# Attention and gated scan on one core: the broadcast of 1/l issued in two halves, the second behind the swap of step 3

## The chip, the core and the metric

The kernel runs on one core of a Trainium2 chip. The metric is the device time of one execution in microseconds (us); the figure given for the kernel before is the median of three executions. Besides it there is one profiled execution, from which every duration of single instructions is taken. The engines are TensorE (PE, with PEld for its weight loads), VectorE (DVE), ScalarE (ACT), GpSimd (POOL) and SyncE (SP), which here only issues DMAs.

## The reference

A batch of 32 sequences of 256 tokens with 128 features passes through two layers, each with a residual.

```python
x = x + attention(layernorm(x), norm_weight, w_qkv, w_out, persist_mem)
x = x + ffn(layernorm(x), ...)
# attention: rms_norm, q, k, v = h @ w_qkv.T, 16 heads of 64, rope on q and k,
# 4 persistent keys and values ahead of the 256, causal softmax, out @ w_out.T
# ffn: over the 32 batches in order,  c = sigmoid(..) * c + sigmoid(..) * tanh(..)
#      h = tanh(x @ wo.T + c_final @ uo.T + bo)
```

The softmax is divided by its row sum l only at the end: the unnormalised product of exp(scores) and v is multiplied by 1/l. The change concerns how 1/l reaches the place of that multiplication.

## The kernel before, in words

**Work and order.** The Python loop `iterations` (L202) runs `body(j, p)` for j = 0 to 34 on each engine, so that each engine has a fixed list of instructions, ordered by hand; engines meet through semaphores only. One iteration has eight steps s = 0 to 7, one for each pair of heads. In iteration j the engines project batch j, do the scores, the softmax and the values of batch j - 1 and j, divide and project out batch j - 2, and run the scan for batch j - 3.

**Rope, one pair of heads a step.** `project` (PE, L1021) makes q and k of one pair in the one PSUM bank `ps_proj`; it waits until DVE has read the pair before. `rotate` (DVE, L793) multiplies the bank by cos into `rope_a` (L798) and by sin into `rope_b` (L799). `rope_b` and `rope_c` have two buffers each, by s % 2. `swap` (SP, L287) waits for the `rope_b` of its step and issues two DMAs that copy the even rows of `rope_b` to the odd rows of `rope_c` and the other way (128 KB each). `rope_add` (POOL, L403) waits for the swap and adds `rope_a` and `rope_c` to `qk`; in the order of POOL the add of pair s - 1 stands in step s, ahead of `prob_add` (L396). `hi` (ACT, L524) casts `qk` to `qk_h`, from which `scores_for_max` (PE, L1060) makes the scores whose row maxima `maxima` (DVE, L801) takes; for pairs 0 to 4 of batch j these run in steps 3 to 7 of iteration j. `transpose_top` (PE, L1077) of step 7 waits for the maxima of step 6. `rotate` of step s waits for the swap of step s - 2 (L797), because it writes the same `rope_b` buffer. So `rotate` of step 5 waits for the landing of the swap of step 3.

**1/l.** In step 1 `invert` (DVE, L828) takes the reciprocal of the row sums of batch j - 2 (L832). In step 2 SP runs `store_linv` (L296), which stores it to a DRAM scratch tensor in two DMAs of 64 KB, then the swap of step 2, then `spread_linv` (L303), which waits for the store to land and for the divisions of the batch before, and issues four DMAs of 256 KB each that read the scratch tensor and write each head's 1/l to the 64 partitions of that head in `rinv`. The first two fill pairs 0 to 3 of `rinv` (semaphore `spread0`), the other two pairs 4 to 7 (`spread1`). The swap of step 3 comes behind the four. `divide` (DVE, L834) multiplies `raw` by `rinv` for two pairs at a time (L845): its first two parts in step 4, behind `spread0`, its last two in step 5, behind the `rotate` of that step and behind `spread1`. `project_out` (PE, L1172) follows in steps 5 and 6. The last batch gets its 1/l through PE (`spread_last`), so there are 31 broadcasts, in iterations 2 to 32; in iteration 32 there is no swap.

**SP's order** in steps 2 and 3 is thus:

```python
if c and s == 2 and j - 2 < NB - 1:
    store_linv(j - 2)
if a:
    swap(j, s)
if c and s == 2 and j - 2 < NB - 1:
    spread_linv(j - 2)
```

After the swap of step 3 comes `tails` (L315), a DMA of 8 KB with the persistent values, and then the swap of step 4. From ACT's queue one batch of x (128 KB) is loaded in each step 4 (L473).

Of the kernel before, what the change touches and what calls it, by code (L numbers as in the profile page):

```python
# [5 lines left out]
NB, NT, D = 32, 256, 128  # L6
# [38 lines left out]
def wait(eng, sem, count):  # L45

    if isinstance(count, int) and count <= 0:
        return
    eng.wait_ge(sem, count)


def build(nc, x, x_last, w_qkv_t, w_out_t, norm_w, pm_k, pm_v, ffn_w, ffn_b, bo_row, consts_f32, consts_cast,
# [9 lines left out]
    with ctx:  # L62
        def sb(name, shape, dt):
            return ctx.enter_context(nc.sbuf_tensor(name, shape, dt))
# [76 lines left out]
        rinv = sb("rinv", [P, NPAIR, NT], f32)  # L141
# [14 lines left out]
        linv_dram = nc.dram_tensor("linv_scratch", [2, 32, 2, NT], f32, kind="Internal").ap()  # L156
# [23 lines left out]
        spread = [S[f"spread{i}"] for i in range(2)]  # L180
# [17 lines left out]
        def real(b):  # L198

            return not isinstance(b, int) or 0 <= b < NB  # L200

        def iterations(eng, body):  # L202


            for j in range(NB + 3):
                body(j, j % 2)

        OWN = (slice(0, 64), slice(64, 128))
# [32 lines left out]
        def fin_x(g):  # L241
            return x_sb[:, FB * g:FB * g + FB, :]
# [20 lines left out]
        @block.sync  # L263
        def _(sp):
            def const_f32(t, name):
                return sp.dma_start(t, consts_f32[:, C32[name][0]:C32[name][1]])

            def load_x(i):
                lo, hi = XCH[i], XCH[i + 1]
                sp.dma_start(x_sb[:, lo:hi, :].rearrange("p b (q d) -> p b q d", q=QT),  # L270
                             x_d[:, lo:hi, :, :]).then_inc(ld_x[i], 16)

            sp.dma_start(x_end[:, :], x_last).then_inc(S["ld_end"], 16)
            load_x(0)
            const_f32(ident_f[:, :], "ident").then_inc(S["ld_ident"], 16)
            sp.dma_start(nw[:, :], norm_w).then_inc(S["ld_ident"], 16)
            sp.dma_start(bias_raw[:, :], ffn_b).then_inc(S["ld_ident"], 16)
            const_f32(cos[:, :], "cos").then_inc(S["ld_rope"], 16)
            const_f32(sin[:, :], "sin").then_inc(S["ld_rope"], 16)
            sp.dma_start(c_raw, consts_cast).then_inc(S["ld_c"], 16)  # L280
            sp.dma_start(pmk_raw[:, :], pm_k).then_inc(S["ld_small"], 16)
            sp.dma_start(bo_sb[:, :], bo_row).then_inc(S["ld_small"], 16)
            const_f32(ones_sum[:, :, :].rearrange("p c n -> p (c n)"), "ones_sum").then_inc(S["ld_small"], 16)
            const_f32(ones_end[:, :, :].rearrange("p e n -> p (e n)"), "ones_end").then_inc(S["ld_small"], 16)
            load_x(1)

            def swap(j, s):  # L287

                sp.wait_ge(S["qk_read"], NPAIR * j + s + 1)
                sp.sem_inc(S["sp_tick"], 1)  # L290
                wait(sp, S["rope_sum"], NPAIR * j + s - 1)
                sp.sem_inc(S["sp_tick"], 1)
                for i in range(2):
                    sp.dma_start(rope_c[i::2, s % 2, :], rope_b[1 - i::2, s % 2, :]).then_inc(swapped[s % 2], 16)

            def store_linv(cj):  # L296

                sp.wait_ge(S["linv_done"], cj + 1)
                sp.sem_inc(S["sp_tick"], 1)
                for b in range(2):  # L300
                    sp.dma_start(linv_dram[:, :, b, :], linv[OWN[b], :]).then_inc(S["linv_stored"], 16)

            def spread_linv(cj):  # L303

                sp.wait_ge(S["linv_stored"], 32 * (cj + 1))
                sp.sem_inc(S["sp_tick"], 1)
                wait(sp, S["norm_done"], 4 * cj)
                sp.sem_inc(S["sp_tick"], 1)
                for half in range(2):
                    for e in range(2):  # L310
                        src = linv_dram[e:e + 1, 2 * half:2 * half + 2, :, :].rearrange("o k b n -> o (k b n)")
                        sp.dma_start(rinv[OWN[e], 4 * half:4 * half + 4, :].rearrange("p s n -> p (s n)"),  # L312
                                     src.to_broadcast([64, 4 * NT])).then_inc(spread[half], 16)

            def tails(bj, half):  # L315

                col = half * DI // 2
                sp.wait_ge(S["v_done"], 4 * bj + 2 * half + 1)
                sp.sem_inc(S["sp_tick"], 1)
                sp.dma_start(v_sb[0:NPM, 0, col:col + DI // 2], pm_v[:, col:col + DI // 2]).then_inc(v_pm[half], 16)  # L320

            def tail_values(bj):

                wait(sp, S["pv_ready"], NPAIR * bj)
                sp.sem_inc(S["sp_tick"], 1)
                if bj == 0:
                    sp.wait_ge(S["ve_stored"], 16)
                    sp.wait_ge(S["casts_pool"], 14)
                for half in range(2):
                    src = v_end_dram[NEND * bj:NEND * bj + NEND, half * DI // 2:(half + 1) * DI // 2]  # L330
                    sp.dma_start(v_end[HB * half:HB * half + KE, :],
                                 src.rearrange("k (s n) -> s k n", s=NPAIR // 2)).then_inc(S["v_end"], 16)

            def body(j, p):
                a, b, c = real(j), real(j - 1), real(j - 2)
                for s in range(NPAIR):
                    if c and s == 2 and j - 2 < NB - 1:
                        store_linv(j - 2)
                    if a:
                        swap(j, s)  # L340
                    if c and s == 2 and j - 2 < NB - 1:
                        spread_linv(j - 2)
                    if j == 1 and s == 3:
                        sp.wait_ge(S["ve_copied"], 2)
                        sp.dma_start(v_end_dram, raw[:, 1, 0:4, :].rearrange("p c n -> p (c n)")).then_inc(S["ve_stored"], 16)
                    if b and s == 3 and j < NB:
                        tails(j - 1, 1)
                    if b and s == 5:
                        tail_values(j - 1)
                    if a and s == 6:  # L350
                        tails(j, 0)

            iterations(nc.sync, body)
            for g in range(NB // FB):
                sp.wait_ge(S["fin_out"], g + 1)
                sp.dma_start(out_d[:, FB * g:FB * g + FB, :, :],
                             fin_x(g).rearrange("p b (q d) -> p b q d", q=QT)).then_inc(S["stored"], 16)
            sp.wait_ge(S["stored"], 16 * (NB // FB))
# [1093 lines left out]
```

## Time and profile before

| what | value |
|---|---|
| median of three executions | 1133.06 us (1131.0 to 1133.95) |
| the profiled execution's own time | 1133.03 us |
| its span in the profile | 1131.2 us |
| mean granted TensorE clock | 0.988 of full speed |
| PE, DVE, ACT, POOL busy | 95%, 82%, 62%, 56% of the span |
| DMA traffic | 120.52 MB, mean 107 GB/s |

A row of the timeline gives the start in us from the start of the span, the duration in us, the engine, the line, the operation with output and inputs, and the number of instructions merged into it; in square brackets stands how long the engine had been idle before it and what released it. SPq is SyncE's queue of DMA instructions: its durations are those of issuing, and the time to landing is told apart. The windows give the length of each window and the busy time of PE, PEld, DVE, ACT and POOL with the number of instructions, then PE's clock, the DMA share and GB/s. A row of the waits gives the total in us, the number of times and the longest. L numbers are lines of the kernel.

### The profile page before, as it was taken

To read this page: it belongs to the slowest core of one execution; us is meant where nothing else is said; L and a number is where in the kernel's file an instruction comes from. 1 tells how busy PE (TensorE), PEld (TensorE's weight loads), DVE (VectorE), ACT (ScalarE), POOL (GpSimd) and SP (SyncE) were. 2 spreads that over 40 slices of the span, in tenths; PEclk is the share of its full clock that TensorE was granted. 3 is DMA by queue.
4 is the path that set the end of the run, shared out by engine and by line. 5 is a ranking of instruction groups with operands and counts; after the bars stand their busy time and mean duration, and the time that the engine had idled before them with its cause. 6 is when DMAs were issued, how large, how long until landed. Compare 5 with 4: busy or idle time off the path is not lost.

```text
span 1131.2 us, 47261 instructions
## 1 busy us (share of the span) xinstructions
PE 1080.3 (95%) x18443; PEld 813.6 (72%) x18443; DVE 930.0 (82%) x3305; ACT 698.4 (62%) x1575; POOL 634.8 (56%) x816
## 2 busy tenths in 40 slices
PE   3879999999999999999999999999999999999996
PEld 2457777777777776777777777677777777777784
DVE  5778888888888888888888888788888888888745
ACT  3556666666666666666666666666665666666644
POOL 3545665576565647656555665555565565556420
PEclk8889999999999999999999999999999999999999
DMA  6213343332333442233333233333323333332215
GB/s 204 95 62 112 111 115 114 115 95 89 111 111 114 115 114 90 90 111 115 115 115 115 83 100 115 107 114 115 115 78 98 114 115 111 108 112 92 68 36 150
DMA packets 78031, 120.52 MB, mean 107 GB/s; under 512 B 13041, under 2 KB 35954, under 8 KB 77682
## 3 DMA queue, kind: packets, MB, share of 16 engines
q1 hardware_dynamic: 68714, 111.20, 32.5%
q10 hardware_dynamic: 9096, 6.30, 2.1%
q8 instruction: 147, 2.41, 1.0%
q14 instruction: 74, 0.61, 0.2%
HBM read 41.56 MB, written 8.78 MB: 45 GB/s over the span
## 4 chain that ended last, share of the span: by engine, by line
PE 59%; DVE 16%; DMA 14%; SPq 4%; issue 3%; POOL 2%; ACT 1%; DVEq 0%; POOLq 0%
PE bank_pv L1142 11%; PE bank L1034 11%; DMA rope_c<-rope_b 10%; PE bank_st L1098 8%; PE bank_sum L1179 5%; PE bank_sum L1163 4%; DVE masked L809 4%; PE bank_sm L1073 4%; PE bank L1056 3%; DMA linv_scratch<-linv 3%; SPq L312 3%; DVE linv L832 2%; DVE rope_a L798 2%; PE bank L1281 2%; PE bank L1283 2%
## 5 line engine op out<-in xcount | busy, mean ns | idle before, releaser
L407 POOL TENSOR_TENSOR qk<-rope_a,rope_c 128x512 f32<-128x512 f32 x256 | 341.0, 1332 | 312.9 <-DMA rope_c<-rope_b 288.9
L809 DVE CUSTOM_DVE_ANT_0 masked<-bank_sm,mask_q 128x132 bf16<-128x132 f32 (+1 forms) x1024 | 307.1, 355 | 17.7 <-PE bank_sm L1073 17.2
L798 DVE TENSOR_TENSOR rope_a<-bank,cos 128x512 f32<-128x512 f32 x256 | 174.1, 680 | 130.1 <-PE bank L1034 83.7
L400 POOL TENSOR_TENSOR prob<-prob 128x264 f32<-128x264 f32 x256 | 210.8, 823 | 117.1 <-ACT prob L544 108.3
L529 ACT ACTIVATE qk_h<-qk 128x512 f16<-128x512 f32 x256 | 160.4, 627 | 172.2 <-POOL qk L407 171.7
L544 ACT ACTIVATE prob<-bank_st 128x784 f32<-128x784 f32 x256 | 209.3, 817 | 59.7 <-PE bank_st L1107 58.9
L1142 PE MATMUL bank_pv<-prob,v_sb 128*64 128x256 f32 (+1 forms) x2048 | 224.8, 340 | 0.6 <-DVE raw L825 0.6
L1098 PE MATMUL bank_st<-qk 64*64 64x256 f32 (+3 forms) x4096 | 186.3, 299 | 0.4 <-issue 0.2
L1098 PEld LDWEIGHTS bank_st<-qk 64*64 64x64 f32 x4096 | 167.7, 134 | 9.6 <-issue 1.3
L799 DVE TENSOR_TENSOR rope_b<-bank,sin 128x512 f32<-128x512 f32 x256 | 173.8, 679 | 0.0
L1142 PEld LDWEIGHTS bank_pv<-prob,v_sb 128*64 128x64 f32 x2048 | 124.3, 136 | 54.4 <-issue 0.9
L1034 PE MATMUL bank<-h_hi,w_hi 128*128 128x256 f16 x512 | 143.5, 280 | 5.8 <-DVE rope_b L799 5.0
L1034 PE MATMUL bank<-h_hi,w_lo 128*128 128x256 f16 x512 | 141.8, 277 | 0.0
L1034 PE MATMUL bank<-h_lo,w_hi 128*128 128x256 f16 x512 | 141.6, 277 | 0.0
L1179 PE MATMUL bank_sum<-wo_sb,raw 128*128 128x128 f32 x992 | 122.7, 276 | 0.0
L1179 PEld LDWEIGHTS bank_sum<-wo_sb,raw 128*128 128x128 f32 x992 | 116.0, 192 | 1.9 <-DVE raw L845 1.1
L578 ACT ACTIVATE v_sb<-bank 128x512 f32<-128x512 f32 x128 | 75.8, 593 | 48.2 <-PE bank L1053 28.7
L569 ACT ACTIVATE raw<-bank_pv 128x256 f32<-128x256 f32 x256 | 97.7, 382 | 4.1 <-PE bank_pv L1148 3.1
L845 DVE SCALAR_TENSOR_TENSOR raw<-rinv,raw 128x512 f32<-128x512 f32 x124 | 96.6, 819 | 2.0 <-DMA rinv<-linv_scratch 1.8
L1073 PEld LDWEIGHTS bank_sm<-qk_h 64*64 64x64 f16 x2048 | 37.6, 105 | 82.7 <-issue 56.6
L1073 PE MATMUL bank_sm<-qk_h 64*64 64x68 f16 (+3 forms) x2048 | 86.7, 246 | 4.4 <-ACT qk_h L529 3.1
L809 DVE DVE_READ_ACCUMULATOR2_ANT top<- 128x1 bf16 x1024 | 85.7, 84 | 0.1
(237 smaller groups left out, 1732.1 us busy)
## 6 DMA issues: line engine op xcount, KB each, us to landing
rope_c<-rope_b SPq DMA_DIRECT2D x512, 128.0 KB, 2.3
rinv<-linv_scratch SPq DMA_DIRECT2D x124, 256.0 KB, 4.8
out<-x_sb SPq DMA_DIRECT2D x16, 256.0 KB, 3.7
linv_scratch<-linv SPq DMA_DIRECT2D x62, 64.0 KB, 2.1
x_sb<-x ACTq DMA_DIRECT2D x28, 128.0 KB, 5.5
xt<-w_qkv_t ACTq DMA_DIRECT2D x1, 1024.0 KB, 5.3
v_end<-v_end_scratch SPq DMA_DIRECT2D x64, 8.0 KB
v_sb<-pm_v SPq DMA_DIRECT2D x63, 8.0 KB
```

The lines of the kernel that those rows point to most:

```text
L400: G.tensor_tensor(prob_2[:, s % 4, :, :], prob[:, s % 4, :, 0:NT - Q1], prob[:, s % 4, :, C0 + Q1:SCOL], ALU.add).then_inc(S["prob_added"], 1)
L407: G.tensor_tensor(qk[:, s, :].rearrange("p (u n) -> p u n", u=2)[:, :, 0:NT], rope_a[:, (NPAIR * j + s) % 3, :].rearrange("p (u n) -> p u ...
L529: A.activation(qk_h[:, s, :].rearrange("p (u n) -> p u n", u=2)[:, :, 0:NT], qk[:, s, :].rearrange("p (u n) -> p u n", u=2)[:, :, 0:NT], A ...
L544: A.activation(prob[:, s % 4, :, :], ps_st[:, :, 0:SCOL], ACT.Exp).then_inc(S["exp_done"], 1)
L798: V.tensor_tensor(rope_a[:, (NPAIR * j + s) % 3, :], proj_bank(j, s)[:, :], cos[:, :], ALU.mult)
L799: V.tensor_tensor(rope_b[:, s % 2, :], proj_bank(j, s)[:, :], sin[:, :], ALU.mult).then_inc(S["qk_read"], 1)
L809: ins = V.tensor_tensor_reduce(masked[:, e, c0:c0 + n], ps_sm[:, e, c0:c0 + n], mask_q[:, c0:c0 + n], 1.0, LOWEST, ALU.add, ALU.max, top[: ...
L1034: last = T.matmul(proj_bank(j, s)[:, u * NT:(u + 1) * NT], W[q][:, col:col + P], H[p][:, par, NPM:NKEY], start=(i == 0), stop=(i == 2))
L1073: last = T.matmul(ps_sm[OWN[SIDE[qb]], e, c0:c0 + n], qk_h[OWN[e], s, qb * HB:qb * HB + HB], qk_h[OWN[e], s, NT:NT + n], start=True, stop= ...
L1098: T.matmul(ps_st[OWN[SIDE[kb]], e, st_cols(blk)], qk[OWN[e], s, NT + kb * HB:NT + kb * HB + HB], qk[OWN[e], s, q0:NT], start=(kc == 0), st ...
L1142: last = T.matmul(ps_pv[OWN[e], q0:NT], v_sb[:, kc, col:col + DH], prob[:, s % 4, e, c0:c0 + NT - q0], start=(kc == 0), stop=(kc == 1))
L1179: last = T.matmul(y_out(cj)[:, q * D:(q + 1) * D], raw[:, par, s, q * P:(q + 1) * P], wo_sb[:, s, :], start=(alone and s == 0 and q == 0), ...
```

## The change

`spread_linv` gets a second argument, `half`, and issues only the two DMAs of that half. SP calls it twice in an iteration: for half 0 behind the swap of step 2, as before, and for half 1 behind the swap of step 3. Both calls keep the two waits and the two semaphore increments. The number of DMAs, their sizes, their semaphores and every other engine's program are the same.

```diff
-            def spread_linv(cj):
+            def spread_linv(cj, half):
 
                 sp.wait_ge(S["linv_stored"], 32 * (cj + 1))
                 sp.sem_inc(S["sp_tick"], 1)
                 wait(sp, S["norm_done"], 4 * cj)
                 sp.sem_inc(S["sp_tick"], 1)
-                for half in range(2):
-                    for e in range(2):
-                        src = linv_dram[e:e + 1, 2 * half:2 * half + 2, :, :].rearrange("o k b n -> o (k b n)")
-                        sp.dma_start(rinv[OWN[e], 4 * half:4 * half + 4, :].rearrange("p s n -> p (s n)"),
-                                     src.to_broadcast([64, 4 * NT])).then_inc(spread[half], 16)
+                for e in range(2):
+                    src = linv_dram[e:e + 1, 2 * half:2 * half + 2, :, :].rearrange("o k b n -> o (k b n)")
+                    sp.dma_start(rinv[OWN[e], 4 * half:4 * half + 4, :].rearrange("p s n -> p (s n)"),
+                                 src.to_broadcast([64, 4 * NT])).then_inc(spread[half], 16)
...
                     if a:
                         swap(j, s)
-                    if c and s == 2 and j - 2 < NB - 1:
-                        spread_linv(j - 2)
+                    if c and s in (2, 3) and j - 2 < NB - 1:
+                        spread_linv(j - 2, s - 2)
```

## Rows read from the trace of the kernel before

**Rows 1.** The page: busy tenths of PE in 40 slices of the span.

```profile
PE   3879999999999999999999999999999999999996
```

**Rows 2.** Busy time by window, one iteration each, from reciprocal to reciprocal.

```profile
408.79:443.76 34.97, 32.81 (x569) 24.64 (x568) 28.77 (x103) 21.09 (x49) 19.94 (x25) 1.00 0.36 101
509.08:541.63 32.55, 32.52 (x572) 24.73 (x568) 27.90 (x105) 21.07 (x49) 19.74 (x25) 1.00 0.37 112
```

**Rows 3.** Timeline of DVE: the reciprocal that opens iterations 2 and 31.

```profile
80.30 1.75 DVE L832 RECIPROCAL linv<-bank_sum 128x256 f32<-128x256 f32 x1
...
1037.35 1.75 DVE L832 RECIPROCAL linv<-bank_sum 128x256 f32<-128x256 f32 x1
```

**Rows 4.** Waits: DVE, 80.3 to 1037.3; SP, whole span; DVE, 1068 to 1089.

```profile
DVE rope_a L798 <- DMA rope_c<-rope_b: 41.8, 29, 3.1
...
SPq L306 <- DMA linv_scratch<-linv: 13.9, 31, 2.0
...
DVE raw L845 <- DMA rinv<-linv_scratch: 1.4, 1, 1.4
```

**Rows 5.** Timeline of SP's queue in the iteration that opens at 509.08.

```profile
512.25 1.13 SPq L294 DMA_DIRECT2D rope_c<-rope_b  x2
513.70 2.40 SPq L312 DMA_DIRECT2D rinv<-linv_scratch  x4
516.28 2.19 SPq L294 DMA_DIRECT2D rope_c<-rope_b  x2
519.18 6.14 SPq L294 DMA_DIRECT2D rope_c<-rope_b  x4
```

**Rows 6.** Timeline of DVE and PE, the same iteration.

```profile
514.74 0.68 DVE L799 TENSOR_TENSOR rope_b<-bank,sin 128x512 f32<-128x512 f32 x1
...
522.77 0.69 DVE L798 TENSOR_TENSOR rope_a<-bank,cos 128x512 f32<-128x512 f32 x1 [1.24 <-DMA rope_c<-rope_b]
523.98 1.84 DVE L845 SCALAR_TENSOR_TENSOR raw<-rinv,raw 128x512 f32<-128x512 f32 x2
...
530.18 0.11 PEld L1081 LDWEIGHTS bank_sm<-ident_b,top 128*128 128x128 bf16 x2 [0.18 <-DVE top L809]
```

**Rows 7.** DVE, PE: first, three latest, last of 29 rotations of step 5.

```profile
93.93 0.69 DVE L798 TENSOR_TENSOR rope_a<-bank,cos 128x512 f32<-128x512 f32 x1 [1.71 <-DMA rope_c<-rope_b]
...
424.91 0.69 DVE L798 TENSOR_TENSOR rope_a<-bank,cos 128x512 f32<-128x512 f32 x1 [2.98 <-DMA rope_c<-rope_b]
...
426.26 0.28 PE L1034 MATMUL bank<-h_hi,w_hi 128*128 128x256 f16 x1 [1.32 <-DVE rope_b L799]
...
722.76 0.69 DVE L798 TENSOR_TENSOR rope_a<-bank,cos 128x512 f32<-128x512 f32 x1 [3.13 <-DMA rope_c<-rope_b]
...
854.85 0.69 DVE L798 TENSOR_TENSOR rope_a<-bank,cos 128x512 f32<-128x512 f32 x1 [2.27 <-DMA rope_c<-rope_b]
...
1017.99 0.69 DVE L798 TENSOR_TENSOR rope_a<-bank,cos 128x512 f32<-128x512 f32 x1 [0.61 <-DMA rope_c<-rope_b]
```

**Rows 8.** By line: the DMAs to `rinv`, over the span.

```profile
L312 SPq DMA_DIRECT2D rinv<-linv_scratch x124: 467/597/1810, 84.9 to 1074.8; - x124
...
DMA to landing us min/median/max: 3.5/4.8/6.9
```

**Rows 9.** By line: the swaps of steps 2 and 3, same iteration.

```profile
L294 SPq DMA_DIRECT2D rope_c<-rope_b x2: 488/542/596, 512.2 to 512.8; - x2
...
DMA to landing us min/median/max: 2.0/2.0/2.1
...
L294 SPq DMA_DIRECT2D rope_c<-rope_b x2: 599/1073/1547, 516.3 to 517.9; - x2
...
DMA to landing us min/median/max: 4.8/4.9/5.1
```

**Rows 10.** Busy time in a window of 1 us of the same iteration.

```profile
517.00:518.00 1.00, 1.00 (x10) 0.30 (x7) 0.85 (x3) 1.00 (x3) 0.83 (x1) 1.00 1.13 254
```

**Rows 11.** Timeline of SP's queue, the iteration that opens at 408.79.

```profile
415.13 2.40 SPq L312 DMA_DIRECT2D rinv<-linv_scratch  x4
```

## The prediction

> **What bounds the kernel now.** I read the page first: PE is at nine tenths or more in 36 of 40 slices [rows 1], so a change to a queue of DMAs can only win where PE stands still. The next view is busy time by window, with the reciprocal of step 1 (L832) as the mark of an iteration. A quiet iteration lasts 32.55 us and holds 32.52 us of PE; its clock column reads 1.00, the upper level of 2.4 GHz. The iteration from 408.79 lasts 34.97 us with hardly more PE work in it, 32.81 [rows 2]. So 32.55 is PE's floor, and what stands above it is waiting. From the first mark at 80.30 to the one at 1037.35 there are 29 iterations [rows 3]: 957.05 us, against 29 x 32.55 = 943.95. The excess is **13.1 us**, 1.2% of the time, and it is all that the steady part has to give.
>
> The waits of DVE say where it arises. `rope_a` of L798 waits for the DMA into `rope_c` 29 times in these 29 iterations, 41.8 us in all [rows 4]: once in each, at the rotation of step 5, which needs the swap of step 3. In SP's queue that swap stands behind four broadcast DMAs [rows 5]. Its `rope_b` was done at 514.74 + 0.68 = 515.42 [rows 6], but it was issued only at 516.28, and landed 4.8 to 5.1 us after issue where the swap of step 2 took 2.0 [rows 9]: ahead of it lie 4 x 256 KB, and the 16 DMA engines are full (share 1.13, 254 GB/s) [rows 10]. It lets the rotation of step 5 go at 522.77, 13.69 us into the iteration [rows 2, 6].
>
> Is that late enough for PE? From the rotation DVE goes on to two divisions at 523.98, a cast and the maxima, and PE's transpose at 530.18 waits 0.18 us for them [rows 6]: just at the edge. I took the start of the step-5 rotation less the mark for each of the 29 iterations, and set it beside each iteration's length. They fit one line: nothing up to 13.86 us, then one us of length for each us of lateness. The three latest are 424.91 - 408.79 = 16.12, 722.76 - 706.39 = 16.37 and 854.85 - 839.40 = 15.45 [rows 2, 7] (the marks 706.39 and 839.40 are read as those of [rows 3]), with 2.26, 2.51 and 1.59 above 13.86; the first of these shows 2.42 above the floor by its window [rows 2]. In it PE also waits openly, 1.32 us at L1034 for DVE's `rope_b` [rows 7]. Summed over all 29 (the first is 93.93 - 80.30 = 13.63, the last 13.32) the part above 13.86 is **12.4 us** of the 13.1. The other 0.7 comes before step 5 or from elsewhere, and the change does not touch it.
>
> **The change, part by part.** *The swap of step 3 moves up.* Half 0 keeps its place: two of four issues, half of 2.40, so 1.20 us from 513.70 to 514.90 [rows 5]. SP then waits for `rope_b` until 515.42 and issues at about 515.6 instead of 516.28, 0.7 us earlier. Ahead of it are 512 KB less; at 254 GB/s [rows 10] that is 2.1 us. It should land some 2.8 us earlier, 10.9 us into a quiet iteration, and in the three late ones at 12.7 to 13.6, all under 13.86. The rotation of step 5 then waits for PE's projection alone, which ended 1.24 us before it in the quiet iteration [rows 6]. So this part alone is worth the whole 12.4.
>
> *Half 1 moves down.* Its two issues come behind the swap (1.13 us, as that of step 2 [rows 5]) and start at about 515.6 + 1.13 + 0.15 = 516.9 instead of 514.9, 2.0 us later; the second starts 0.6 us after the first, at 517.5, 8.4 us into the iteration. Who waits is the division of step 5, on DVE behind the rotation, and behind it the cast, the maxima and the rotation of step 6. In the kernel before it starts 1.21 us after the rotation [rows 6], so its own edge is 13.86 + 1.21 = **15.07 us** into the iteration: what half 1 lands later than that costs one for one. The trace does not show that landing in the new order, so I bound it. Low end: the median of the broadcasts, 4.8 us from issue [rows 8], gives 8.4 + 4.8 = 13.2 in a quiet iteration and at most 14.5 in one whose store of 1/l was late: no cost. High end: the longest of the broadcasts, 6.9 us [rows 8], in every iteration: 15.3 to 16.6, over 29 iterations 14.1 us. I take a value between, from the nearest row: the same bytes (four broadcasts and one swap) go through the same full engines, only in another order, so the last of them lands when the last landed before, and that was the swap of step 3, whose landing is the start of the step-5 rotation. The 29 starts against 15.07 leave 1.05 + 1.30 + 0.38 = **2.7 us**, from the three latest alone [rows 7].
>
> *Also moved past on SP's queue.* The small `tails` DMA and the swap of step 4 (519.18 [rows 5]) come after the same number of issues as before; SP reaches them at the same time, and the swap waits for its `rope_b` anyway. POOL's and ACT's work behind the swap of step 3 gets earlier, which frees nothing on PE. The second call adds two waits that are already met and two semaphore increments, some 0.1 us of SP, which is idle for most of an iteration: nothing. It also looks once more at the store of 1/l (13.9 us of waiting in 31 times before [rows 4]); the first call has waited for it, so the second never does. That wait is why the broadcast starts 6.34 us into the iteration at 408.79 [rows 11] against 4.62 [rows 5], and it stays. In iteration 32 there is no swap, the four DMAs go out in a row as before, and DVE's 1.4 us there [rows 4] stays.
>
> *A rule to weigh.* The rows of the broadcasts and swaps show the swap slow behind four broadcasts and quick without them, as if the queue were served in order. The Trainium skill, page "DMA: Bandwidth & Descriptors", section "Two DMAs through the same engine are not ordered", says that descriptors start in order but are pipelined, and that nothing orders DMAs across the 16 engines. By the first reading half 1 cannot delay a swap issued ahead of it; if the second went so far that all five DMAs ended together, the swap would gain nothing, which is the first rival.
>
> The sum: 12.4 - 2.7 = 9.7 us off the profiled execution, 1133.03 - 9.7 = 1123.3 us. That execution lies 0.03 us below the median of the three runs, so no correction is needed.
>
> **The rivals.** A measurement of this kernel can tell about 0.3%, or 3.4 us, from no change.
>
> *The burst lands as one.* Half 1 follows the swap within 0.2 us and shares all DMA engines; if they mix, the swap lands with the last of the burst, as before, and the excess stays: 1133. For it: the engines are full, and the swap of step 4 already shares them. Against it: the swap of step 3 lands later than the broadcasts issued before it. Between this and the forecast lies a part: swap and half 1 both middling late.
>
> *Everything goes.* Half 1 lands by the median, the 2.7 us vanish too: 1133.0 - 12.4 = 1120.6.
>
> *Slower: half 1 becomes the late one.* The wait moves from L798 to L845 on DVE, and the maxima and PE's transpose follow. It decides from the landing of half 1's second DMA: at 6.9 us from issue the loss of 14.1 is 1.7 more than the gain of 12.4, so break-even is a little under that. At 7.4 us, half a us over the longest seen, it costs 29 x 0.99 = 28.7, net 16.3: 1149. For it: it is issued 2.0 us later into engines that are already full, and the swap of step 4 and the load of x come close behind. Against it: the bytes ahead of it grow only by a swap, and those behind it in the queue came late before, too.
>
> *The change does nothing*, because half 1 was never ahead of the swap in effect, is excluded by the rows: four issues stand before it [rows 5].
>
> **How the numbers follow.** Forecast with half 1's leftover between 0 and about 6 us, 1120.5 to 1126.5, "everything goes" among it: 0.70 (of this the lower end, 1120.6, 0.25). Gain between 3.4 and 6 us: 0.07. Burst as one, or a part gain within 3.4 us, or half 1 at the longest landing (1134.7): 0.15. Slower: 0.08. So faster 0.77, same 0.15, slower 0.08. The predicted time is that of the likeliest, 1123.3. The range begins at 1119.8, just under the floor of 1120.6 by what single runs scatter, and must reach past the part gains to 1129.6, where the 0.3% ends; 0.77 lies inside, and a little more for the edge: 1119.8 to 1130.0.
>
> **What would show it.** Right: in SP's queue two broadcasts, a swap 6.5 us into the iteration, two broadcasts; the rotation of step 5 at about 12.5 us, released by PE; the wait of L798 for `rope_c` down from 41.8 us to near nothing; a wait of L845 for `rinv` in few iterations, of a few us in all; 29 iterations in some 946 to 948 us. Wrong: L798 still released by the swap in most iterations (burst as one), or L845 waiting for `rinv` in most and the transpose of L1081 waiting behind it (slower). If the 29 iterations still take over 953 us with both waits gone, the line of 13.86 us was not the cause of the excess.

## The result and the profile after

The changed kernel is not faster but, by a small margin that is clear of the scatter, slower: 1135.46 us in the median of 20 runs (1131.27 to 1139.43) against 1131.98 us of the kernel before in 20 runs (1129.68 to 1134.92), a ratio of 1.0026 with an interval of 1.0013 to 1.0038. The forecast was 1123.3 us, and the range ended at 1130.0.

The profiled execution of the changed kernel happens to be the fastest of its 20, 1131.27 us with a span of 1129.5. A second one was taken in the first experiment.

The page, busy shares of the engines:

```profile
PE 1082.0 (96%) x18443; PEld 815.3 (72%) x18443; DVE 956.6 (85%) x3305; ACT 703.9 (62%) x1575; POOL 631.5 (56%) x816
```

PE does what it did. VectorE runs the same 3305 instructions and is busy for 956.6 us; on the page of before it was 930.0 (82%). Nothing was added to VectorE's program, and yet 26.6 us of busy time came in. That is the first thing to look at.

The waits of DVE from 80.3 to 1037.3 us, which answer to [rows 4]:

```profile
DVE raw L844 <- DMA rinv<-linv_scratch: 6.8, 11, 1.0
DVE rope_a L797 <- DMA rope_c<-rope_b: 0.9, 2, 0.7
```

The wait that the prediction went after is gone, 41.8 us down to 0.9, and the new wait for half 1 is small, 11 times and 6.8 us. Both are as forecast. Still the 29 iterations between the first and the last mark, which answer to [rows 3], take 954.19 us against 957.05:

```profile
80.19 1.75 DVE L831 RECIPROCAL linv<-bank_sum 128x256 f32<-128x256 f32 x1
...
1034.38 1.75 DVE L831 RECIPROCAL linv<-bank_sum 128x256 f32<-128x256 f32 x1
```

That is 10.2 us above the floor of 29 x 32.55 (the excess of the prediction), and this is the best execution. In the second profiled one it was 12.8, and 13.1 in the kernel before. The prediction had named this sign: over 953 us with both waits gone, and lateness past its line of 13.86 us is not the cause of the excess. Indeed the step-5 rotations are late by only 4.9 us in all beyond that line, read as in the prediction, against 12.4 before.

SP's queue in the iteration that opens at 377.20, the answer to [rows 5]:

```profile
383.70 1.13 SPq L294 DMA_DIRECT2D rope_c<-rope_b  x2
385.01 1.11 SPq L311 DMA_DIRECT2D rinv<-linv_scratch  x2
...
387.29 1.13 SPq L294 DMA_DIRECT2D rope_c<-rope_b  x2
```

And the landing of the second DMA of the swap of step 3 and of half 1, by line in windows that hold one DMA each, the answer to [rows 8, 9]:

```profile
L294 SPq DMA_DIRECT2D rope_c<-rope_b x1: 597/597/597, 384.2 to 384.2; - x1
DMA to landing us min/median/max: 4.9/4.9/4.9
...
L311 SPq DMA_DIRECT2D rinv<-linv_scratch x1: 597/597/597, 385.5 to 385.5; - x1
DMA to landing us min/median/max: 6.3/6.3/6.3
```

The swap goes out 6.50 us into the iteration and lands at 384.2 + 4.9 = 389.1, 11.9 us in; half 1 lands at 385.5 + 6.3 = 391.8, 14.6 us in, just before its edge of 15.07. So the queue does what the change says. The order was kept where it mattered: the swap was complete 2.7 us before the half that was issued behind it, and in all 29 iterations it was so by 1.7 us or more. Over the 29 the swap is complete 11.8 us into the iteration on average (14.0 before) and half 1 at 14.5; half 1 passes 15.07 in six of them, by 2.4 us in all.

What DVE and GpSimd did with it, timelines of the same iteration put together in order of time, the answer to [rows 6]:

```profile
388.17 1.28 DVE L844 SCALAR_TENSOR_TENSOR raw<-rinv,raw 128x512 f32<-128x512 f32 x2
389.27 1.31 POOL L406 TENSOR_TENSOR qk<-rope_a,rope_c 128x512 f32<-128x512 f32 x1 [3.62 <-DMA rope_c<-rope_b]
389.38 1.49 DVE L903 SCALAR_TENSOR_TENSOR c<-ga,gb 128x256 f32<-128x256 f32 x1
390.54 0.93 POOL L399 TENSOR_TENSOR prob<-prob 128x264 f32<-128x264 f32 x1
390.79 0.68 DVE L797 TENSOR_TENSOR rope_a<-bank,cos 128x512 f32<-128x512 f32 x1
391.39 0.68 DVE L798 TENSOR_TENSOR rope_b<-bank,sin 128x512 f32<-128x512 f32 x1
391.98 2.36 DVE L844 SCALAR_TENSOR_TENSOR raw<-rinv,raw 128x512 f32<-128x512 f32 x2
392.43 1.36 POOL L406 TENSOR_TENSOR qk<-rope_a,rope_c 128x512 f32<-128x512 f32 x1 [0.96 <-DMA rope_c<-rope_b]
```

The swap lands, GpSimd starts its rope add at 389.27, and the state update of the scan (L903) that VectorE starts 0.11 us later lasts 1.49 us. The rotation of step 5 shows no wait: it stands behind that update, and begins at 390.79, 13.59 us into the iteration, hardly before the 13.69 of the quiet iteration in [rows 6]. The two divisions behind it take 2.36 us with the next rope add beside them, where the undisturbed pair at 388.17 takes 1.28. The same operations grouped by line and shape, from 80.3 to 1037 us, of the kernel before and then of the changed one (count, busy us, mean ns, idle before them):

```profile
L845 DVE SCALAR_TENSOR_TENSOR raw<-rinv,raw 128x512 f32<-128x512 f32 x116 | 90.5, 821 | 0.5 <-DMA rinv<-linv_scratch 0.4
...
L904 DVE SCALAR_TENSOR_TENSOR c<-ga,gb 128x256 f32<-128x256 f32 x28 | 11.6, 415 | 0.0
```

```profile
L844 DVE SCALAR_TENSOR_TENSOR raw<-rinv,raw 128x512 f32<-128x512 f32 x116 | 100.1, 903 | 7.2 <-DMA rinv<-linv_scratch 6.8 <-issue 0.2
L903 DVE SCALAR_TENSOR_TENSOR c<-ga,gb 128x256 f32<-128x256 f32 x28 | 26.1, 934 | 0.0
```

The update went from 415 to 934 ns, the division from 821 to 903. The rotation, which reads its first input from PSUM, is 680 ns before and 678 after, though GpSimd runs beside it too (`prob_add` at 390.54).

### The profile page after: what moved, and what is told of

It is laid out like the page before. It is cut to its first block, busy times and chain, and to the rows that moved or that the text cites. A ratio compares the mean times of both kernels' runs of the same rounds, so it can differ in the third digit from the quotient of the medians.

```text
span 1129.5 us, 47323 instructions
## 1 busy us (share of the span) xinstructions
PE 1082.0 (96%) x18443; PEld 815.3 (72%) x18443; DVE 956.6 (85%) x3305; ACT 703.9 (62%) x1575; POOL 631.5 (56%) x816
## 4 chain that ended last, share of the span: by engine, by line
PE 73%; DVE 16%; DMA 4%; issue 3%; SPq 1%; POOL 1%; ACT 1%; DVEq 0%; POOLq 0%
PE bank_pv L1141 14%; PE bank L1033 13%; PE bank_st L1097 10%; PE bank_sum L1178 7%; PE bank_sum L1162 5%; PE bank_sm L1072 5%; DVE masked L808 4%; PE bank L1055 4%; DVE raw L844 3%; PE bank L1280 3%; PE bank L1282 3%; PE bank L1052 2%; PE bank_st L1101 2%; DVE rope_a L797 2%; DMA v_sb<-pm_v 2%
## 5 line engine op out<-in xcount | busy, mean ns | idle before, releaser
L399 POOL TENSOR_TENSOR prob<-prob 128x264 f32<-128x264 f32 x256 | 207.7, 811 | 142.5 <-ACT prob L543 136.1
L798 DVE TENSOR_TENSOR rope_b<-bank,sin 128x512 f32<-128x512 f32 x256 | 173.7, 678 | 0.0
L844 DVE SCALAR_TENSOR_TENSOR raw<-rinv,raw 128x512 f32<-128x512 f32 x124 | 106.5, 898 | 8.3 <-DMA rinv<-linv_scratch 8.0
```

The lines of the kernel that those rows point to most:

```text
L399: G.tensor_tensor(prob_2[:, s % 4, :, :], prob[:, s % 4, :, 0:NT - Q1], prob[:, s % 4, :, C0 + Q1:SCOL], ALU.add).then_inc(S["prob_added"], 1)
L798: V.tensor_tensor(rope_b[:, s % 2, :], proj_bank(j, s)[:, :], sin[:, :], ALU.mult).then_inc(S["qk_read"], 1)
```

## The experiments

Two theories stood after this. **Port theory:** the rope add of pair 3 on GpSimd, set free early, holds up VectorE operations that read two tensors from SBUF, the memory that both engines work on, and these stand ahead of the rotation. (The name is that of a supposed cause, a shared way into that memory; the runs can show the hold-up, not the port.) **Late-half theory:** half 1 is what costs. All edits are to the changed kernel unless said otherwise.

**The changed kernel again** (no edit).

> The changed kernel as it is, for a second profiled execution and as the control of this call. Both theories: within 1131 to 1139 us, some 0.3% above the kernel before. Port theory (GpSimd's rope add of pair 3 now runs while VectorE divides and updates the scan state, and the one holds up the other): the state update of step 4 (L903) has a mean of 900 ns or more against 415 before, and the rotation of step 5 starts at 13.5 us or later in most iterations though its swap has landed. Late-half theory (half 1 lands too late for the division of step 5): VectorE waits for rinv at L844 in most iterations, over 10 us in all.

Measured: 1133.99 us (12 runs), ratio 1.0019, 0.9999 to 1.0038. The state update has 934 ns again, and the step-5 rotation starts 13.66 us into an iteration on average (14.15 in the kernel before), in 19 of 29 iterations at 13.5 or later. VectorE waited for `rinv` 10 times, 7.4 us. This is the port theory on every count; the wait for the late half stays under the 10 us that its theory asked for.

**GpSimd held until the state update is done.**

```diff
+                    if s == 4 and real(j - 3) and a:
+                        pool.wait_ge(S["dve_s"], 3 * (j - 3) + 3)
                     if s >= 1 and a:
                         rope_add(j, s - 1)
```

> The changed kernel with one more wait: GpSimd starts the rope add of step 4 only when VectorE has finished the state update of step 4. Port theory: the state update falls back to 415 to 450 ns, the rotation of step 5 starts at 12.4 to 12.7 us, the excess over 32.55 us an iteration falls to 2 to 5 us, and the time to 1122 to 1126 us, 0.6 to 0.9% under the kernel before. Late-half theory: the excess stays at 10 to 14 us and the time at 1133 to 1137, for nothing is done about the landing of half 1.

Measured: **1125.69 us** (7 runs), ratio 0.9949, 0.9927 to 0.9971. One more wait makes the kernel faster. By line:

```profile
L905 DVE SCALAR_TENSOR_TENSOR c<-ga,gb 128x256 f32<-128x256 f32 x28 | 11.6, 413 | 0.0
```

By wait, 80.3 to 1037.3 us:

```profile
DVE raw L846 <- DMA rinv<-linv_scratch: 16.5, 25, 1.6
```

The update is back at 413 ns and the rotation starts at 12.78 us on average, a little later than the 12.4 to 12.7 forecast. Now that VectorE is early it does wait for `rinv`, 25 times, nearly always for half 1; but the excess, 7.6 us, is more than the 2 to 5 forecast, and the divisions of step 5 still last up to 2.9 us for the pair. The time lies inside the forecast, near its upper end.

**No half 1** (its two DMAs left out, the last two divisions read the first half).

```diff
-                    if c and s in (2, 3) and j - 2 < NB - 1:
-                        spread_linv(j - 2, s - 2)
+                    if c and s == 2 and j - 2 < NB - 1:
+                        spread_linv(j - 2, 0)
...
-                if n % 2 == 0:
-                    dve.wait_ge(spread[n // 2], 32 * (cj + 1))
-                V.scalar_tensor_tensor(o, rinv[:, 2 * n:2 * n + 2, :], 1.0, o, ALU.mult, ALU.mult).then_inc(S["norm_done"], 1)
+                if n == 0:
+                    dve.wait_ge(spread[0], 32 * (cj + 1))
+                V.scalar_tensor_tensor(o, rinv[:, 2 * (n % 2):2 * (n % 2) + 2, :], 1.0, o, ALU.mult, ALU.mult).then_inc(S["norm_done"], 1)
```

> The changed kernel without the DMAs of half 1: the last two divisions read the first half of rinv, so the results of heads 8 to 15 are divided by the sums of heads 0 to 7 and nothing waits for half 1. Late-half theory: the excess goes, 1120 to 1123 us. Port theory: the stretched state update and divisions stay (L902 or L903 at 900 ns), the rotation of step 5 stays at 13.5 us in most iterations, and the time stays above 1127 us.

Measured: 1133.0 us (12 runs), ratio 1.0004, 0.9987 to 1.0021. With half of the broadcasts gone and nobody waiting for them, the kernel is no faster than before the change. The late-half theory, 1120 to 1123 us, falls here. What half 1 costs this run can't say, for it changes a second thing: the swap is complete earlier still, 11.2 us into an iteration on average instead of 11.8, and the collisions get worse:

```profile
L844 DVE SCALAR_TENSOR_TENSOR raw<-rinv,raw 128x512 f32<-128x512 f32 x116 | 107.7, 967 | 0.1
L903 DVE SCALAR_TENSOR_TENSOR c<-ga,gb 128x256 f32<-128x256 f32 x28 | 31.1, 1111 | 0.0
```

**The kernel before, with one more GpSimd operation at that place,** whose result nobody reads.

```diff
+                    if s == 4 and c and a:
+                        pool.wait_ge(S["max_done"], NPAIR * j + 2)
+                        G.tensor_tensor(idle[:, :], cos[:, :], sin[:, :], ALU.add)
                     if s >= 1 and a:
                         rope_add(j, s - 1)
```

> The kernel BEFORE with one added GpSimd operation in step 4 of iterations 2 to 31: an add of cos and sin (128x512) into a buffer that nobody reads, started when the maxima of step 4 are done, just where the changed kernel's rope add of pair 3 falls. Port theory: the divisions of step 4 and the state update behind them stretch together by about 1 us an iteration (the update from 415 to about 900 ns), but the rotation behind them waits for its swap until 13.7 us anyway, so the time grows by 0 to 3 us only. If there is no such hold-up, both durations stay as they were.

Measured: 1142.46 us (4 runs), ratio 1.0107, 1.0074 to 1.014. The timelines of the iteration that opens at 543.66:

```profile
554.63 2.36 DVE L849 SCALAR_TENSOR_TENSOR raw<-rinv,raw 128x512 f32<-128x512 f32 x2
554.78 1.65 POOL L442 TENSOR_TENSOR idle<-cos,sin 128x512 f32<-128x512 f32 x1 [2.68 <-DVE top L813]
...
556.91 0.41 DVE L908 SCALAR_TENSOR_TENSOR c<-ga,gb 128x256 f32<-128x256 f32 x1
```

This is the hold-up by itself: no data passes between the added operation and the divisions, and the pair of divisions goes from 1.28 to 2.36 us (2.22 to 2.37 over the 29 iterations). That stretch was forecast; for the update, 900 ns were forecast and 490 measured, because the pair, twice as long, had mostly taken the whole collision. The time was not forecast: by the ratio it grew by some 12 us, by the medians taken together 10.2 (1132.28 to 1142.46), not 0 to 3. The mark-to-mark excess went from 13.1 to 20.4 us. Iterations that were at the floor now stand at 0.21 us above it, for PE's second pair of output projections waits for the second division of step 4; I had looked at the rotation as the only way from a late division to PE. And in seven iterations the pair of step 5 takes 2.9 us as well. The waits agree, PEld's row over the whole span, where the kernel before has 1.1 us, 6 times:

```profile
PEld bank_sum L1183 <- DVE raw L849: 7.7, 19, 0.7
```

**Both collisions held off.** To the wait above a second one, before the rope add of step 5:

```diff
+                    if s == 5 and c and a:
+                        pool.wait_ge(S["norm_done"], 4 * (j - 2) + 4)
```

> The changed kernel with two waits on GpSimd: the rope add of step 4 after VectorE's state update (as in e2_pool_held), and the rope add of step 5 after the last division of batch j-2. Port theory, as it stands now: the pair of divisions of step 5 took up to 2.9 us in e2_pool_held instead of 1.28 because the rope add of pair 4 ran beside it; with it held they take 1.3 us unless they wait for rinv, the excess falls from 7.6 to 2 to 5 us and the time to 1120 to 1124 us. Rival (what is left in e2_pool_held is the late landing of half 1): the time stays at 1125 to 1127 us.

Measured: **1122.65 us** (8 runs), ratio 0.9918, 0.9892 to 0.9945: 0.8% faster than the kernel before, the best of the variants that keep both halves. Divisions, update and the wait for half 1:

```profile
L848 DVE SCALAR_TENSOR_TENSOR raw<-rinv,raw 128x512 f32<-128x512 f32 x117 | 80.9, 730 | 17.0 <-DMA rinv<-linv_scratch 16.7
...
L907 DVE SCALAR_TENSOR_TENSOR c<-ga,gb 128x256 f32<-128x256 f32 x28 | 11.6, 412 | 0.0
```

The excess is 2.5 us, and the pair of divisions of step 5 takes 1.48 us on average and never over 1.93. VectorE still waits 16.7 us in all for `rinv`, but in room that it has.

**The second wait alone, in the kernel before.**

> The kernel BEFORE with the second of these waits alone: the rope add of step 5 starts after the last division. Port theory: the pair of divisions of step 5 falls from 1.83 to 1.28 us, the edge behind which a late rotation of step 5 costs time moves from 13.86 to about 14.4 us, and of the 12.4 us of excess 5.7 are left: 1124 to 1128 us. If only the landing of the step-3 swap matters, nothing changes: 1131 to 1133 us.

Measured: 1132.46 us (12 runs), ratio 1.0018, 0.9996 to 1.004: no change, and the 1124 to 1128 us of the port theory missed. The forecast named the wrong partner. In the iteration that opens at 474.54 the pair of divisions of step 5 still takes 1.84 us, and what runs beside it is not the rope add of pair 4 but `prob_add`, let go by the late rope add of pair 3:

```profile
489.67 1.27 POOL L407 TENSOR_TENSOR qk<-rope_a,rope_c 128x512 f32<-128x512 f32 x1 [6.18 <-DMA rope_c<-rope_b]
490.26 0.68 DVE L801 TENSOR_TENSOR rope_b<-bank,sin 128x512 f32<-128x512 f32 x1
490.86 1.84 DVE L847 SCALAR_TENSOR_TENSOR raw<-rinv,raw 128x512 f32<-128x512 f32 x2
490.90 1.25 POOL L400 TENSOR_TENSOR prob<-prob 128x264 f32<-128x264 f32 x1
```

Here both sides are stretched at once, 1.84 against 1.28 and 1.25 against 0.75. `rope_b` of the same engine, which reads PSUM, keeps its 0.68 beside GpSimd's add.

**The second wait alone, in the changed kernel.**

> The changed kernel with the second wait alone, so that the rope add of pair 3 still runs beside the divisions and the state update of step 4. Port theory: the collision in step 5 goes, that of step 4 stays and keeps the rotation of step 5 at 13.5 us or later in most iterations; the time lies between e5_hold_both and the changed kernel, 1125 to 1131 us. Rival (the collision of step 4 costs nothing, only that of step 5 does): as e5_hold_both, within 1 us.

Measured: 1129.51 us (12 runs), ratio 0.9987, 0.9966 to 1.0007. Between the two, as the port theory says. The profile is of the slowest of the 12 runs, 1133.61 us: the update stays at 992 ns, the rotation starts at 13.83 us on average, and PE waits for divisions. By line, and by wait over the span:

```profile
L905 DVE SCALAR_TENSOR_TENSOR c<-ga,gb 128x256 f32<-128x256 f32 x28 | 27.8, 992 | 0.0
```

```profile
PE bank_sum L1180 <- DVE raw L846: 4.9, 9, 0.8
```

**Both waits and no half 1** (the edits of the fifth and of the third experiment together).

> e5_hold_both without the DMAs of half 1; the last two divisions read the first half of rinv, so heads 8 to 15 are divided by the wrong sums. The difference to e5_hold_both is what the landing of half 1 costs. Port theory: 1 to 3 us less than e5_hold_both, so 1119 to 1121 us, at the floor. Late-half theory: 5 us less or more.

Measured: 1122.48 us (6 runs), ratio 0.9919, 0.9888 to 0.995, the same as with half 1. So with GpSimd held off the late landing of half 1 costs nothing that can be measured, less than the 1 to 3 us forecast; the excess is 1.9 us against 2.5. Not every collision is gone in these two kernels. The wait holds the rope add of pair 4, and not the `prob_add` before it, which meets the divisions of step 5 in nearly every iteration here:

```profile
778.37 1.94 DVE L848 SCALAR_TENSOR_TENSOR raw<-rinv,raw 128x512 f32<-128x512 f32 x2
778.56 1.20 POOL L399 TENSOR_TENSOR prob<-prob 128x264 f32<-128x264 f32 x1
```

With the rotation at 12.5 us that lengthening has room: this iteration lasts 32.54 us, which is the floor.

**Both waits in the kernel before,** the control.

> The kernel BEFORE with both waits of e5_hold_both on GpSimd, as its control: all four broadcasts stand ahead of the swap of step 3. Port theory: in the kernel before, the rope add of pair 3 starts after the state update anyway, because its swap lands late; the waits change nothing and the time is that of the kernel before within 3 us. Rival (the gain of e5_hold_both comes from the waits and not from the early swap): 1122 to 1125 us.

Measured: 1132.55 us (12 runs), ratio 0.9987, 0.9965 to 1.0009. The waits alone win nothing that can be told from the scatter, because the late swap had kept GpSimd away already; the rotation still waits for the swap:

```profile
DVE rope_a L802 <- DMA rope_c<-rope_b: 36.0, 28, 2.1
```

**Both waits, and both halves behind the swap of step 3.**

```diff
-                    if c and s in (2, 3) and j - 2 < NB - 1:
-                        spread_linv(j - 2, s - 2)
+                    if c and s == 3 and j - 2 < NB - 1:
+                        spread_linv(j - 2, 0)
+                        spread_linv(j - 2, 1)
```

> e5_hold_both, but with BOTH halves behind the swap of step 3. The swap is as early as it can be and the broadcasts are as late: half 0 is issued 7.8 us into an iteration instead of 4.6 and should land after the divisions of step 4 want it (11.0 us). If a late half costs as soon as it passes its edge: VectorE waits for rinv at the first division for 0.5 to 2 us in most iterations, PE behind it, and the time is 1125 to 1131 us. If there is room for late halves: within 1.5 us of e5_hold_both.

Measured: 1198.42 us (6 runs), ratio 1.0571, 1.0537 to 1.0604. The direction was forecast, the size was not: 76 us over the kernel with both waits, where 1131 us would have been 8. The wait forecast with it, 0.5 to 2 us in most of 29 iterations, would alone make up to 15 to 58 us if PE had to sit it out. VectorE's and PE's waits, over the stretch from 80.3 to 1037.3 us and from 100 to 1040:

```profile
DVE raw L849 <- DMA rinv<-linv_scratch: 67.9, 33, 3.8
...
PE bank_sum L1183 <- DVE raw L849: 48.3, 26, 3.6
```

The divisions of the iteration that opens at 502.09, timeline of VectorE:

```profile
515.00 1.29 DVE L849 SCALAR_TENSOR_TENSOR raw<-rinv,raw 128x512 f32<-128x512 f32 x2 [1.04 <-DMA rinv<-linv_scratch]
518.38 1.45 DVE L849 SCALAR_TENSOR_TENSOR raw<-rinv,raw 128x512 f32<-128x512 f32 x2 [0.56 <-DMA rinv<-linv_scratch]
```

The divisions start 12.9 and 16.3 us into the iteration, and PE stands at the output projection behind them. Part of the size is PE's clock. In the iteration that opens at 256.12 PE stands still for 2.51 us before that projection, and then works on the lower level of its clock, 1.2 GHz: the granted clock reads 1.00 up to 272, 0.51 and 0.50 in the next two windows of 1 us, and 1.00 again from 276. Timeline of PE, then those two windows, then this iteration beside the next one:

```profile
271.16 3.03 PE L1183 MATMUL bank_sum<-wo_sb,raw 128*128 128x128 f32 x16 [2.51 <-DVE raw L849]
...
272.00:273.00 1.00, 1.00 (x7) 1.00 (x7) 1.00 (x3) 0.00 (x0) 0.88 (x1) 0.51 0.02 6
273.00:274.00 1.00, 1.00 (x6) 0.89 (x5) 1.00 (x3) 0.58 (x2) 1.00 (x2) 0.50 0.00 0
...
256.12:293.03 36.91, 34.37 (x572) 26.17 (x568) 28.56 (x103) 21.25 (x49) 19.20 (x25) 0.95 0.31 96
293.03:327.16 34.13, 32.77 (x572) 24.72 (x568) 28.39 (x105) 21.11 (x49) 19.25 (x25) 1.00 0.34 103
```

The same 572 matmuls take 1.6 us more. Nine of the 29 iterations read 0.95; by that difference it is an estimated 14 us of the 76. So the broadcasts do have an edge, sharp for half 0, and the changed kernel is on the safe side of it.

**The state update behind the rotation** instead of ahead of it, no added wait.

```diff
-                    if s == 4 and d and j != NB + 1:
-                        state(j - 3, 1)
...
+                    if s == 5 and d and j != NB + 1:
+                        state(j - 3, 1)
                     if s == 5 and c and j - 2 < NB - 1:
                         divide(j - 2, p, 2)
```

> The changed kernel without any added wait, but VectorE runs the state update of step 4 behind the rotation of step 5 instead of ahead of it. Port theory: one of the two operations that the rope add of pair 3 can hold up no longer stands before the rotation; the rotation starts at 12.2 to 13.3 us, and the time lies between e2_pool_held and the changed kernel, 1124 to 1131 us. Rival (the delays of the rotation come from elsewhere): 1133 to 1137 us as the changed kernel.

Measured: 1131.32 us (12 runs), ratio 0.9978, 0.9961 to 0.9994. A little faster than before, just past its interval, and 0.3 us above the 1124 to 1131 forecast. The rotation starts at 13.1 us on average, as forecast. Taking one of the victims out of the way helps less than keeping GpSimd away from all: the update is at 715 ns, the division now at 951, and PE waits for it:

```profile
PE bank_sum L1178 <- DVE raw L844: 4.2, 8, 1.2
```

## Why the prediction was wrong

**The floor and the excess** were right. With GpSimd held off, the steady part came down to 2.5 us above the 943.95 that the prediction called its floor.

**The swap of step 3** was right in kind: issued at 6.50 us as forecast, landing 11.9 us into the iteration instead of 10.9 (11.8 on average), and the wait of L798 gone.

**Half 1** was right in its landing and on the cautious side in its cost. It landed past 15.07 us by 2.4 us in all, against 2.7 forecast, though in six iterations and not three. But with both waits, leaving half 1 out altogether changed the time from 1122.65 to 1122.48 us only. In the changed kernel the same cut left 1133.0 against 1133.99 us, with worse collisions, so there its cost stays open.

**The step that failed** is one clause among the things moved past: "POOL's and ACT's work behind the swap of step 3 gets earlier, which frees nothing on PE". It was costed at nothing because it gains nothing. I asked what an earlier rope add would release, and not what it would run beside. It runs beside the divisions and the state update of VectorE, which start at 388.17 and 389.38, 10.97 and 12.18 us into the iteration shown, and in the kernel before had GpSimd idle beside them, because the swap landed at 13.7. The price: the update by 934 - 415 = 519 ns on average, the division by 82; 28 x 0.519 + 116 x 0.082 = 24 us of VectorE's time, most of the 26.6 that the page shows. "The rotation of step 5 then waits for PE's projection alone" was therefore false: it waited for VectorE itself, and started at 13.6 us instead of the 12.5 forecast.

A misread row helped to hide this. The 1.24 us in [rows 6] is the idle time of VectorE before the rotation, and not the time since PE's projection ended. It began when VectorE's own state update ended; the projection was done before that, timelines of DVE and PE in the kernel before:

```profile
521.12 0.42 DVE L904 SCALAR_TENSOR_TENSOR c<-ga,gb 128x256 f32<-128x256 f32 x1
521.12 0.27 PE L1034 MATMUL bank<-h_lo,w_hi 128*128 128x256 f16 x1
```

So the 12.5 us was the end of the update from the start, and whatever lengthens the update moves the rotation.

The edges went too: both 13.86 and 15.07 were read from a kernel in which the pair of divisions of step 5 took 1.83 or 1.84 us in each of the 29 iterations. In the changed one it takes 1.28 to 2.92, on average 1.81, so a fixed edge no longer describes it. And the lateness has a second way to PE, by the second division of step 4, which the prediction did not have; the added GpSimd operation in the kernel before showed it.

With GpSimd held off, the change gives about what was forecast for it: 0.9918 of the time before, 9.3 us of 1132 (8.4 by the medians, 10.6 by the 29 iterations of the two profiles), against the 9.7 of the sum. Of the 13.1 us of excess the prediction would have left 3.4, and 2.5 were left. The size of the DMA part was about right, and was taken back whole by a part that the sum did not hold.

**The trace of before had a sign of it.** In the quiet iteration of [rows 6] the pair of divisions at 523.98 takes 1.84 us, and the pair at 519.91 takes 1.29; the prediction used the first number as a duration and did not ask why it is longer. Beside it GpSimd's `prob_add` runs for 1.25 us instead of 0.75, timelines of the kernel before:

```profile
519.91 1.29 DVE L845 SCALAR_TENSOR_TENSOR raw<-rinv,raw 128x512 f32<-128x512 f32 x2
...
524.02 1.25 POOL L400 TENSOR_TENSOR prob<-prob 128x264 f32<-128x264 f32 x1
```

The rule for it stands in the Trainium skill, page "SBUF — State Buffer", section "Who interferes with whom": a VectorE instruction with two SBUF inputs contends with a GpSimd instruction that reads SBUF, the later one blocks until the other is done, and one with at most one SBUF input, outside the 2-port modes, does not contend. The traces agree: the update and the divisions read two SBUF tensors, and beside a rope add of 1.28 us the update of the iteration shown grew by 1.08 us and the pair of divisions by 1.08; the rotations read PSUM and cos or sin and stay at 678 to 680 ns. No run here moved an operand from one memory to the other, so that it is the second SBUF input that decides is read off from which operations stretch.

**The rivals.** "The burst lands as one" did not happen, the swap landed 2.7 us ahead of half 1. The slower rival, half 1 as the late one, ended on the right side of the result by the wrong mechanism: VectorE waited 6.8 us for `rinv`, not in most iterations but 11 times, and the run without half 1 was not faster than the kernel before. The case that came true, a collision of two engines because one of them starts earlier, was among none of them.

The changed kernel seems to scatter more (1131.27 to 1139.43) than the one before (1129.68 to 1134.92), but nothing has to be explained there: in 24 later runs the kernel before went from 1127.57 to 1139.83. Not settled is what the time depends on within one kernel: whether a rope add meets the update or just misses it hangs on some tenths of a microsecond of a landing, and no run was made for that alone.

## What to carry to other kernels

When a wait goes away, list not only what the released work lets go, but also what it will now run beside, above all on VectorE and GpSimd: an idle gap on one of them may be what keeps the other fast. When the same instruction has two durations in a trace, look at the other engine before using either as a price. When a row shows a gap, ask whose gap it is: what stood before it on the same engine may be the next thing to wait for. And where a released operation has slack, as the rope add had here, hold it back with a wait until the sensitive operations have passed; here that turned a loss of 0.3% into a gain of 0.8%.

## What the runs showed of the hardware that was not expected

- A GpSimd add that reads SBUF and shares no operand with the VectorE divisions beside it lengthened the pair of them from 1.28 to 2.36 us, and the add itself, 1.65 us there, is longer than the 1.27 of a rope add of the same shape that runs undisturbed. The time spent held up is shown as busy time of both instructions, not as idle: VectorE's busy time grew by 26.6 us with the same instructions.
- On SyncE's queue, transfers made of two DMAs were complete in the order of their issue also with the DMA engines full (shares of 0.99 to 1.14 from 384 to 390), in all 29 iterations of the changed kernel: in the one shown the swap at 4.9 us from issue, half 1 behind it at 6.3. Single DMAs did overtake: in 25 of the 29 the first DMA of the swap of step 4 landed before the second DMA of half 1, issued ahead of it (there 387.3 + 3.6 = 390.9 against 391.8).
- Half 0 issued 7.8 instead of 4.6 us into the iteration, and half 1 behind it, took the kernel with both waits from 1122.65 to 1198.42 us. A halt of PE of 2.51 us there was followed by work at half clock, so the halt cost more than its own length.
